# Products of constants in TensorE's pauses, ahead of the attention and in the second routing of a MoE, attention, MoE layer

## The reference

```python
x = x + 0.5 * ffn(layernorm(x))      # gate: top 2 of 8 experts; silu(x w0) * (x w1), then wo; 256 -> 512 -> 256
x = x + attention(layernorm(x))      # 16 heads, latent queries and keys of rank 64, 64 plain + 64 rotary features
x = x + 0.5 * ffn(layernorm(x))      # the same weights as in the first line
```

## Time and profile before

| | |
|---|---|
| median of 3 runs | 1137.31 us (1135.53 to 1138.65) |
| the profiled execution | 1136.86 us, of which the span is 1135.0 |
| mean granted TensorE clock | 0.959 |
| TensorE busy | 1012.5 us (89%) |
| VectorE, ScalarE, GpSimd busy | 715.5, 522.4, 444.2 us |
| TensorE instructions | 6200, with 6201 weight loads |

### The profile page before, as it was taken

One profiled execution on the slowest core, in us unless ns is written; L12 is line 12 of the kernel. 1 busy time (PEld: TensorE's weight loads), 2 busy tenths in 40 slices (PEclk: granted clock), 3 DMA queues, 4 the chain that ended last, 5 costly groups with the idle time before them and its releaser, 6 DMA issues.

```text
span 1135.0 us, 22156 instructions
## 1 busy us (share of the span) xinstructions
PE 1012.5 (89%) x6200; PEld 810.0 (71%) x6201; DVE 715.5 (63%) x1570; ACT 522.4 (46%) x1127; POOL 444.2 (39%) x401
## 2 busy tenths in 40 slices
PE   5669999998369999999999999999989459999994
PEld 4548788887347777777778777777778448778884
DVE  6365656654457788877887787777344545656542
ACT  2243333422146776767767677777210123433321
POOL 2552233233334553646463644443014422233232
PEclk9999999999669999999999999999999679999998
DMA  9843544532100111111111111111654544544330
GB/s 254 254 166 85 125 101 102 111 50 29 56 1 10 57 38 38 39 29 31 36 38 39 38 39 38 39 38 53 219 162 149 200 128 109 156 106 100 51 55 7
DMA packets 71591, 95.80 MB, mean 84 GB/s; under 512 B 9600, under 2 KB 48640, under 8 KB 71296
## 3 DMA queue, kind: packets, MB, share of 16 engines
q1 hardware_dynamic: 57216, 78.04, 22.6%
q0 software_dynamic: 14304, 16.87, 8.4%
HBM read 64.37 MB, written 34.43 MB: 87 GB/s over the span
## 4 chain that ended last, share of the span: by engine, by line
PE 49%; DMA 27%; issue 11%; POOL 3%; DVE 3%; ACT 1%; POOLq 1%; SPq 0%; DVEq 0%; ACTq 0%
DMA out<-shared,small 13%; DMA x_after_moe<-shared,small 13%; PE bank L1625 10%; PE bank L1652 10%; PE bank L1613 5%; PE bank L1614 5%; PE bank L1615 5%; PE bank L1600 2%; POOL rows_by_expert L533 2%; PE bank L1601 2%; PE bank L1731 1%; PE bank L1568 1%; PE bank L1439 1%; PE bank L1441 1%; PE bank L1443 1%
## 5 line engine op out<-in xcount | busy, mean ns | idle before, releaser
L845 ACT ACTIVATE shared<-bank,small 128x512 f32<-128x512 f32 x256 | 176.5, 690 | 95.2 <-DVE small L1266 94.2
L1266 DVE TENSOR_REDUCE small<-bank 128x1 f32<-128x512 f32 x256 | 174.7, 685 | 47.8 <-PE bank L1615 47.5
L777 ACT CAST split_rows_and_inner<-bank 128x512 fp32r<-128x512 f32 x78 | 46.0, 589 | 246.8 <-PE bank L1424 246.8
L1625 PE MATMUL bank<-constants,shared 128*128 128x128 f32 x1024 | 157.0, 276 | 2.0 <-ACT shared L845 0.5
L1625 PEld LDWEIGHTS bank<-constants,shared 128*128 128x128 f32 x1024 | 123.2, 141 | 44.9 <-issue 14.2
L1441 PE MATMUL bank<-expert_weights_low,split_rows_and_inner 128*128 x312 | 143.5, 460 | 0.0
L1443 PE MATMUL bank<-expert_weights_high,split_rows_and_inner 128*128 x312 | 142.4, 456 | 0.0
L1613 PE MATMUL bank<-expert_weights_high,shared_split 128*128 128x512 f32 x256 | 124.7, 487 | 5.9 <-POOL shared_split L589 5.9
L1439 PE MATMUL bank<-expert_weights_high,split_rows_and_inner 128*128 x312 | 125.2, 401 | 2.9 <-DVE split_rows_and_inner L1075 2.5
L1080 DVE TENSOR_TENSOR split_rows_and_inner<-bank,split_rows_and_inner 128x512 fp32r<-128x512 f32 x78 | 53.9, 691 | 113.7 <-ACT split_rows_and_inner L777 113.7
L546 POOL DMA_INDIRECT out<-shared,small x39 | 61.4, 1574 | 149.4 <-DMA out<-shared,small 120.3
(11 more groups left out here) (187 smaller groups left out, 2120.6 us busy)
## 6 DMA issues: line engine op xcount, KB each, us to landing
expert_weights<-L_ffn_w_kernel SPq DMA_DIRECT2D x32, 512.0 KB, 5.0
shared<-rows_by_expert SPq DMA_DIRECT2D x78, 129.0 KB, 2.1
expert_weights<-L_ffn_wo_kernel SPq DMA_DIRECT2D x16, 512.0 KB, 6.3
shared<-inverse_sums SPq DMA_DIRECT2D x64, 128.0 KB, 2.9
attended_transposed<-shared SPq DMA_DIRECT2D x32, 256.0 KB, 3.0
expert_weights<-x_after_moe SPq DMA_DIRECT2D x8, 512.0 KB, 4.8
expert_weights<-attended_transposed SPq DMA_DIRECT2D x2, 2048.0 KB, 11.2
shared<-attended_transposed SPq DMA_DIRECT2D x2, 2048.0 KB, 10.9
```

Of the source, the lines that this page charges most:

```text
L845: nc.scalar.activation(prob[k % 4], bank[k % 4][:, :], ACT.Exp, bias=negmax[:, k % 8:k % 8 + 1], accum_out=psum[par][:, hh * GT + qt:hh * ...
L1266: V.tensor_reduce(negmax[:, k % 8:k % 8 + 1], bank[k % 4][:, :], AX.X, ALU.max, negate=True).then_inc(max_ready, 1)
L1625: last = tr(bank[4 + k % 2][:, c * P:(c + 1) * P], prob[k % 4][:, c * P:(c + 1) * P], ident)
```

## The change

A helper `keep_busy(count, b)` issues `count` fp32 products of the identity with the cosine table into bank `b`. Nobody reads the results, and no semaphore is raised. It is called at six places, 47 products in all: 15 after the first MoE, 5 between the projection and the transposes of the keys, 4 between the queries and the scores of the first pair, 5 ahead of the last sequence's transposes, 2 between its logits and its ranks, and 16 between the counts and the second MoE. The loop over the last three routing parts is written out for that. No other engine's program changes.

```diff
--- before.py
+++ after.py
@@ -1406,6 +1406,11 @@
                 pe.wait_ge(carry_ready[f], NG)
                 mm(bank[3][:, 0:E], ones, carry, start=True, stop=True).then_inc(counts_psum[f], 1)
 
+            def keep_busy(count, b):
+
+                for n in range(count):
+                    mm(bank[b][:, :], ident, cst[:, C_COS:C_COS + S], start=True, stop=True)
+
             def moe(f):
                 def xt(i, k, c):
 
@@ -1553,6 +1558,7 @@
             pe.wait_ge(wa_ready, 1)
 
             moe(0)
+            keep_busy(15, 3)
 
             def turn_rows(g, c, b):
                 pe.wait_ge(xn_ready[1], g + 1)
@@ -1580,6 +1586,7 @@
                 turn_rows(0, c, c)
             for half in range(2):
                 project(0, half, 2 + half)
+            keep_busy(5, 7)
             for n, b in ((0, 4), (1, 6), (2, 5)):
                 turn_keys(0, n, b)
 
@@ -1701,6 +1708,7 @@
 
             for part in range(3):
                 queries(0, 0, part)
+            keep_busy(4, 1)
             scores(0, 0, 0)
             scores(0, 0, 1)
             scores(0, 0, 2)
@@ -1732,9 +1740,13 @@
                                   start=(a == 0), stop=(a == PAIRS - 1))
                     last.then_inc(wo_psum, 1)
                     second_route(g - 1, j)
-            for part in range(3):
-                second_route(NG - 1, part)
+            keep_busy(5, 4)
+            second_route(NG - 1, 0)
+            second_route(NG - 1, 1)
+            keep_busy(2, 4)
+            second_route(NG - 1, 2)
             counts(1)
+            keep_busy(16, 4)
             moe(1)
 
 
```

## The result

The changed kernel took 1124.91 us in the median of 4 runs (1123.03 to 1126.85), against 1137.1 us (1135.53 to 1138.65) before, now in 4 runs: a ratio of 0.9895 with a 95% interval of 0.9876 to 0.9914. Measured again on another chip it was 1124.43 against 1133.99 us, ratio 0.9901 (0.9879 to 0.9922).

What follows compares the result with a forecast made beforehand. Before the attention and in the last routing, a chain over several engines bounds, with TensorE's short pieces as links at half clock. Gains of 5.1 and 1.1 us, total 6.2, gave 1131; range 1125.5 to 1135.5 (8 in 10).

Steps and rivals of the forecast that it cites:

- The cap by VectorE: Before the attention: VectorE normalises rows until 303.06, so faster transposes and projection together gain at most 3.07 us.
- The rival in which products of constants don't hold the clock: The clock falls at 286.7 despite the 15 products after the first MoE, groups run late: about 1155 us, chance 0.06.
- that of no gain: Late products and unphased falls give back the gains, or another engine's chain is the bound: 1137 us, chance 0.15.
- So transposes, logits and ranks don't help to hold 2.4 GHz either, as I read it: Read from the opening, where 21 us of transposes and 8-column products never raised the clock.
- at the edge of what has lost the clock: 2.6 us without dense products before the projection: transposes and projection gain 2.5 us, 1.9 if the clock falls.
- the terms of the logits: Last routing: logits from 3.55 to 1.85 us would give 1.7; 0.9 taken, as the clock falls somewhere there.
- the stretch of the queries: Between the 5 and the 4 added products, some 7 us: the clock falls, queries gain 0.6 of 1.7 us.
- the pause of the first pair: Pause inside the attention's first pair of heads, fall at 337.9: no products added, stays as it is, gain 0.
- The routing: Last routing through the start of the second MoE: 1.1 us gained in sum, bounds -1.3 and 5.7.
- clock falls once more in most phases: Before the second MoE's first expert product, 3.5 us without dense products: the clock falls again, 0.3 us gained.
- the first rival: Clock holds across transposes, queries and logits; both upper bounds hold, 7.7 + 5.7 = 13.4 us: 1124, chance 0.17.
- no fall from 282 to 330: Sign in the profile, from the first MoE's end into the scores, that would prove the forecast wrong: then 1124.

Runs made afterwards that it cites:

- the 8-column kernel: Changed kernel with half-length groups, each product replaced by 4 fp32 products of 8 columns: 1134.67 against 1133.99 us before the change, ratio 0.9997.
- the full-length kernel: Changed kernel with all six groups at full length, each product replaced by 8 transposes of the identity: 1127.32 against 1133.99 us before the change, ratio 0.9921.
- the repeat: The changed kernel as it is, measured again on another chip: 1124.43 against 1133.99 us before the change, ratio 0.9901.
- 19 products: Changed kernel with 19 products instead of 16 before the second MoE: 1123.91 against 1133.53 us before the change, ratio 0.9902.
- 8 late ones: Changed kernel with 8 products instead of 4 between the queries and the scores: 1128.10 against 1133.53 us before the change, ratio 0.9946.

## Why the prediction fell short

**Right.** The clock is what pays. A product costs 0.87 us at full clock (15 in 13.05 us), 0.86 forecast. The groups of 15, 5 and 5 fit with rests of 0.6, 0.9 and 0.85 us, as forecast; the 4 ran in part at half and just fit, the 2 were 0.5 us late, and the 16 ended 0.9 ahead of the rows. The cap by VectorE: the reduction came 6.2 us after the start of the transposes (302.25 - 296.07), where I had said 6.3 to 7.5. The key transposes gave 0.6 (0.5 forecast), the last transposes 0.87. The rival in which products of constants don't hold the clock and that of no gain are both refuted.

**Wrong, first: transposes.** The step that failed is "So transposes, logits and ranks don't help to hold 2.4 GHz either, as I read it". For short products the 8-column kernel bears it out. For transposes it is wrong, both ways: alone they held the clock for 7 us, in the full-length kernel for 13, and raised it within 3.7. The opening, from which I read it, has only groups of 8 transposes of 128 by 128, and one of 16 of 64 by 64, among logits and ranks, and I put the failure of the mixture on both. Part 4 of "TensorE: Matmul & The Clock Gate" in the Trainium skill, which I named beside it, says too that transposes don't count as activity the way products do; the runs here disagree for fp32 transposes of 128 by 128 (7.15 us of them at a grant of 1.00). In the sum it sat in the 2.6 us between the first 15 products and the projection, "at the edge of what has lost the clock": the clock held through them in every one of the profiles with full groups, so transposes and projection gave 3.2 us (3.02 and the late start), not 2.5. Whether the transposes in these 2.6 us held it, or whether they are simply too short, no run separates. So the false reading accounts for 0.7 us there and for part of the terms of the logits; the larger part of the miss lies in the falls that came later than forecast, or not at all: in the two profiles 2.8 us more than forecast were gained ahead of the attention and 3.1 more in the routing, and 1.6 were lost at 799.9.

**Wrong, second: how much the stretch of the queries costs.** I forecast a fall there, and it came, but only during the third query, at 311.9 (with 315.2 the rise). Three terms were mis-sized with it: the queries gave 1.0 (3.62 to 4.60), not 0.6; the four products were not late (0 instead of -0.8); the first scores gave 1.8 (2.0 in the second profile), of 2.3. In all from the first query to the third maximum 2.8 us, where I had 2.1.

**Wrong, third: the pause of the first pair.** I set it to 0 because no product is added there. Before, the clock was at half for 6.8 us behind it; in this profile 3.4, and in four others with full groups not at all (the repeat, the long transposes, 19 products, 8 late ones). It gave 1.3 us (6.42 to 7.69), and 2.8 in the second profile of the full change. How much of that the added products cause is not shown: the kernel with the routing products alone gained 3.2 us at the same place with nothing added ahead of it.

Ahead of the attention: 3.2 + 0.6 + 1.0 + 0 + 1.8 + 1.3 = 7.9 us in the two profiles and 7.7 in the timed runs with this place alone, against 5.1, which lies just outside their interval (5.3 to 10.2).

**The routing.** 1.1 us were forecast, 1.7 timed alone (0.6 to 3.0, so the forecast holds), and 4.2 lie between the two profiles (6.1 to 10.29 in the table). In these the logits came through before the fall (1.6 instead of 0.9); behind them the late products lost 0.3 (8.57 to 8.27, where I had -1.0), which is made up by the first expert product (8.74); and the second MoE started at full clock (1.5 instead of 0.3). The last does not repeat in the two profiles shown above with a pause of over 4 us ahead of the MoE, as my "clock falls once more in most phases" had it.

**The range.** Its lower end went 5.5 of the 7 us from the forecast to the first rival. The rival itself, 13.4 us and 1124, is nearest to the time, with a chance of 0.17. Its premise is half true: transposes hold the clock, short products don't. That it comes so near is in part luck: its own sign, no fall from 282 to 330, was not met (311.9), its routing part of 5.7 us was 1.7 when timed alone, and about 2 us of the whole are in neither part alone. The rows of the opening could not separate the two, and the range should have reached to the rival for that reason.

## What to carry to other kernels

In a kernel whose TensorE has pauses of several us between short pieces on the critical chain, filling the pauses with products that nobody reads gives those pieces full clock at no cost in time: 1% here, 1.4% with more of the gaps filled. Before you read a gain from two profiles, find out how far the falls move by themselves: here that was up to 3.7 us in one stretch. Size a group by its pause at full clock and never beyond it, since a late one can cost its whole overrun (8 instead of 4 products: a first score 3.5 us late, 3.3 of them lost in the profile). Transposes of 128 columns and products of 512 both served; products of 8 columns kept the engine as busy and gained nothing. And when a chain of short pieces seems to prove that a kind of work doesn't count, look whether that kind ever stood alone.

## What was not expected of the hardware

- fp32 transposes of 128 by 128, alone, held 2.4 GHz for 7 and for 13 us, and the clock rose from 1.2 GHz 3.7 us after a run of nothing but them had begun.
- Products of 8 columns with the engine 100% busy: the clock fell at 286.8 and 887.6, as with an idle engine (286.7 and 887.4 to 887.5).
- The page's clock row begins with 9s in the opening although all durations there are those of 1.2 GHz. The kernels with products in the opening show what a real rise and fall there look like (5 in the third slice of the last clock line).
- The clock fell at the last attended product (797 to 812 us, by kernel) in 7 of the 12 profiles of kernels with no edit near it, at 1.6 to 1.7 us each time (5.24 to 5.36 instead of 3.67).
- Without added work ahead of it, the first pair of heads took 3.7 us less in one execution than in another, because the clock rose after 2.9 instead of 5.4 us and did not fall again.
